# Attention A: the high and the low part of a tile's probabilities turned by two DMA transposes in place of one

## The chip, the core and the metric

The kernel runs on one core of one Trainium2 chip. The metric is the device time of one execution in microseconds. The kernel before has a median of 2229.25 us over three runs (2225.32 to 2232.22).

## What is computed

The program is a chain of four residual blocks on `x` of shape (4, 1024, 128): attention A, a feed-forward block on selected tokens, attention B, and the feed-forward block again. The change touches attention A alone:

```python
logits = jnp.einsum('bhid,bhjd->bhij', q, k) * SCALE      # 16 heads of 8, q and k with rope
logits = jnp.einsum('bhij,gh->bgij', logits, Wpre)        # heads are mixed before the softmax
attn = jax.nn.softmax(logits, axis=-1)
attn = jnp.einsum('bhij,gh->bgij', attn, Wpost)           # and after it
out = jnp.einsum('bhij,bhjd->bhid', attn, v)
out = out.transpose(0, 2, 1, 3).reshape(b, n, DIM)
return out @ Wout.T + bout
```

## The kernel before

`prepare_a` makes q, k (split in two f16 parts, `kh` and `kl`) and v. `attend_a` then works through TILES_A = 512 tiles: 4 batches by 16 mixed heads by 8 tiles of 128 queries. A tile T passes through the engines so:

- TensorE, `scores(T)` (L335): six 512-column matmuls (L349, L350, L353) make 128 x 1024 scores in one of two PSUM buffers, `score_ps[T % 2]`. It waits until the exponential of T-2 is done.
- VectorE, `row_max(T)` (L450): the negated row maximum.
- ScalarE, `exponentiate(T)` (L400): the probabilities `probs`, in f32, and their sum.
- ScalarE, `high(T)` (L408): the high f16 part, `parts[:, T % 4, 0, :]`. It waits until the transpose of tile T-4, which reads the same slot of `parts`, has landed.
- VectorE, `low(T)` (L456): what the high part leaves, in f16, into `parts[:, T % 4, 1, :]`, and the semaphore `lo_ready`.
- SyncE (L326 to L332): one DMA transpose (L330) turns both parts, 128 x 2048 f16, that is 524,288 bytes, into `pT[:, T % 8]`. It waits for `lo_ready` of T and for `pv_done` of T-8, which frees the slot of `pT`.
- TensorE, `times_v(T)` (L357): 24 matmuls of 128 columns. For each of 8 key blocks j it takes high by the high part of v (L367), high by the low part of v (L369) and low by the high part of v (L371).
- ScalarE, `evict` (L418), and GpSimd, `weigh` and `add` (L510, L517), scale and sum two tiles at a time.

The rings are 4 slots deep for `probs` and `parts` (RING_P) and 8 for `pT` (RING_T). TensorE issues `scores(T + 8)` ahead of `times_v(T)`. ScalarE's order is `exponentiate(i)`, then `high(i - 1)`; VectorE's is `row_max(i)`, then `low(i - 2)`. Once in eight tiles, ScalarE and VectorE also make the next head's scaled q (L390, L441).

Of the kernel before, what the change touches and what calls it, by code (L numbers as in the profile page):

```python
# [14 lines left out]
NB, SEQ, D = 4, 1024, 128  # L15
# [12 lines left out]
JB = SEQ // P  # L28
# [3 lines left out]
AHEAD_A, RING_T, RING_P = 8, 8, 4  # L32
# [255 lines left out]
def attend_a(st, io, qT, kh, kl, v, wpre, wpost, acc, pw):  # L288
# [5 lines left out]
    with ExitStack() as s:  # L294
        probs = st.sb(s, "a_probs", [P, RING_P, SEQ])
        parts = st.sb(s, "a_parts", [P, RING_P, 2, SEQ], F16)
        pT = st.sb(s, "a_pT", [P, RING_T, 2, JB, P], F16)
# [5 lines left out]
        vs = st.sb(s, "a_vs", [P, NB, 2, JB, D], F16)  # L303
# [5 lines left out]
        vhi_made, vlo_made, weighed_ready = st.sem("a_vhi_made"), st.sem("a_vlo_made"), st.sem("a_weighed_ready")  # L309
        scored, max_ready, exp_done = st.sem("a_scored"), st.sem("a_max_ready"), st.sem("a_exp_done")  # L310
        hi_ready, lo_ready = st.sem("a_hi_ready"), st.sem("a_lo_ready")
        turned = [st.sem(f"a_turned{i}") for i in range(RING_T)]
        pv_done, rden_ready = st.sem("a_pv_done"), st.sem("a_rden_ready")
        evicted, added = st.sem("a_evicted"), st.sem("a_added")
        block = s.enter_context(nc.Block())

        def wait_turned(eng, T):

            eng.wait_ge(turned[T % RING_T], 16 * (T // RING_T + 1))

        @block.sync
        def _(sp):
            sp.dma_start(pw.ident[:], io["ident"]).then_inc(pw.loaded, 16)
            sp.dma_start(pw.wout[:], io["wout_T"]).then_inc(pw.loaded, 16)
            sp.dma_start(pw.bout[:], io["bout"].broadcast_to([P, D])).then_inc(pw.loaded, 16)
            for T in range(TILES_A):  # L326
                if T >= RING_T:
                    sp.wait_ge(pv_done, T - RING_T + 1)
                sp.wait_ge(lo_ready, T + 1)
                sp.dma_start_transpose(pT[:, T % RING_T].rearrange("p a j q -> p (a j) q"),  # L330
                                       parts[:, T % RING_P].rearrange("p a c -> p (a c)")).then_inc(
                    turned[T % RING_T], 16)  # L332

        @block.tensor
        def _(pe):  # L335
            def scores(T):

                if T >= TILES_A:
                    return
                G, t = T // TPB, T % TPB  # L340
                if t == 0:
                    pe.wait_ge(qlo_made, G + 1)
                if T >= 2:
                    pe.wait_ge(exp_done, T - 1)
                out, base = score_ps[T % 2], G // HA * SEQ
                qhi, qlo = qs[:, G % 2, 0, t * P:(t + 1) * P], qs[:, G % 2, 1, t * P:(t + 1) * P]
                for c in range(2):
                    to, kc = out[:, c * CH:(c + 1) * CH], slice(base + c * CH, base + (c + 1) * CH)
                    pe.matmul(to, qhi, kh[:, kc], start=True, stop=False)  # L349
                    pe.matmul(to, qhi, kl[:, kc], start=False, stop=False)  # L350
                for c in range(2):
                    to, kc = out[:, c * CH:(c + 1) * CH], slice(base + c * CH, base + (c + 1) * CH)
                    last = pe.matmul(to, qlo, kh[:, kc], start=False, stop=True)  # L353
                last.then_inc(scored, 1)

            def times_v(T):

                b = T // (HA * TPB)
                if T % (HA * TPB) == 0:
                    pe.wait_ge(vlo_made, b + 1)  # L360
                if T >= 8 and T % 2 == 0:
                    pe.wait_ge(evicted, T - 6)
                wait_turned(pe, T)
                out = out_ps[:, T // 2 % 4, T % 2, :]
                for j in range(JB):
                    hi, lo = pT[:, T % RING_T, 0, j, :], pT[:, T % RING_T, 1, j, :]
                    pe.matmul(out[:, 0:D], hi, vs[:, b, 0, j, :], start=j == 0, stop=False,  # L367
                              skip_group_check=True)
                    pe.matmul(out[:, 0:D], hi, vs[:, b, 1, j, :], start=False, stop=False,  # L369
                              skip_group_check=True)  # L370
                    last = pe.matmul(out[:, 0:D], lo, vs[:, b, 0, j, :], start=False,  # L371
                                     stop=j == JB - 1, skip_group_check=True)
                last.then_inc(pv_done, 1)

            for T in range(AH):
                scores(T)
            for T in range(TILES_A):
                scores(T + AH)
                times_v(T)

        @block.scalar
        def _(act):
            def scale_q(G):

                if G >= heads:
                    return
                if G >= 2:
                    act.wait_ge(scored, TPB * (G - 1))
                b, g = G // HA, G % HA
                act.activation(qs[:, G % 2, 0, :], qT[:, b * SEQ:(b + 1) * SEQ], ACT.Copy,  # L390
                               scale=wpre[:, g:g + 1]).then_inc(qhi_made, 1)

            def exponentiate(T):

                act.wait_ge(max_ready, T + 1)
                if T >= RING_P:
                    act.wait_ge(lo_ready, T - RING_P + 1)
                if T >= 16:
                    act.wait_ge(rden_ready, T // 2 - 7)
                act.activation(probs[:, T % RING_P, :], score_ps[T % 2][:], ACT.Exp,  # L400
                               bias=negmax[:, T % 8:T % 8 + 1], accum_out=den[:, T % 16:T % 16 + 1]).then_inc(exp_done, 1)

            def high(T):

                act.wait_ge(exp_done, T + 1)
                if T >= RING_P:
                    wait_turned(act, T - RING_P)
                act.activation(parts[:, T % RING_P, 0, :], probs[:, T % RING_P, :], ACT.Copy,  # L408
                               scale=PSCALE).then_inc(hi_ready, 1)

            def evict(pair):

                act.wait_ge(rden_ready, pair + 1)
                act.wait_ge(pv_done, 2 * pair + 2)
                if pair >= 2:
                    act.wait_ge(weighed_ready, pair - 1)
                for T in (2 * pair, 2 * pair + 1):
                    act.activation(own_out[:, T % 4, :], out_ps[:, pair % 4, T % 2, 0:D], ACT.Copy,  # L418
                                   scale=rden[:, T % 16:T % 16 + 1]).then_inc(evicted, 1)

            scale_q(0)
            scale_q(1)
            for i in range(TILES_A + AH + 2):
                if i >= AH + 2 and i % 2 == 0:
                    evict((i - AH - 2) // 2)
                if i < TILES_A:
                    exponentiate(i)
                if 1 <= i <= TILES_A:
                    high(i - 1)
                if i % TPB == 1 and i < TILES_A:  # L430
                    scale_q(i // TPB + 1 if i >= TPB else heads)

        @block.vector
        def _(dve):
# [18 lines left out]
            def low(T):  # L453

                dve.wait_ge(hi_ready, T + 1)
                dve.scalar_tensor_tensor(out=parts[:, T % RING_P, 1, :], in0=probs[:, T % RING_P, :], scalar=PSCALE,  # L456
                                         in1=parts[:, T % RING_P, 0, :], op0=ALU.mult,
                                         op1=ALU.subtract).then_inc(lo_ready, 1)
# [11 lines left out]
            for i in range(TILES_A + AH + 2):  # L470
                if i < TILES_A:
                    row_max(i)
                if 4 <= i < TILES_A + 4 and i % 2 == 0:
                    invert((i - 4) // 2)
                if 2 <= i < TILES_A + 2:
                    low(i - 2)
                if i % TPB == 3 and TPB <= i < TILES_A:
                    low_q(i // TPB + 1)
# [1109 lines left out]
def build(nc, io, out):  # L1588
    with ExitStack() as whole:
# [4 lines left out]
        with ExitStack() as s:  # L1594
            acc = st.sb(s, "acc", [P, NT, D])
            pw = ProjectWeights(st, s)
            with ExitStack() as held:
                qT = st.sb(held, "qT", [P, NTOK])
                kh = st.sb(held, "kh", [P, NTOK], F16)
                kl = st.sb(held, "kl", [P, NTOK], F16)  # L1600
                v = st.sb(held, "v", [P, NTOK])
                wpre = st.sb(held, "wpre", [P, HA])
                wpost = st.sb(held, "wpost", [P, HA * D])
                ident = st.sb(held, "a_ident", [P, P])
                prepare_a(st, io, x, qT, kh, kl, v, wpre, wpost, ident)
                attend_a(st, io, qT, kh, kl, v, wpre, wpost, acc, pw)
            project_a(st, x, acc, pw, lstats, fw)
# [85 lines left out]
```

## Time and profile before

| | |
|---|---|
| median of three runs | 2229.25 us (2225.32 to 2232.22) |
| the profiled execution: its time | 2227.8 us |
| the profiled execution: its span | 2225.9 us |
| mean granted TensorE clock | 0.979 of 2.4 GHz |
| attention A's tiles, first to last DMA transpose issued | 76.6 to 1472.9 us |
| DMA transposes | 512 |

The profile comes from one execution, so a sum over its rows is made against its own 2227.8 us and then carried over to the median, which is 1.45 us longer. In the profile, DVE is VectorE, ACT is ScalarE, POOL is GpSimd, PE is TensorE, PEld its weight load, and SP is SyncE; a q behind an engine's name is its instruction queue. Instructions that only issue a DMA are not counted as busy, so the first part of the page says nothing about SP.

### The profile page before, as it was taken

The page shows a single profiled execution, that of the slowest core. Times are in us where ns is not written, and L with a number is a line of the kernel's source. Part 1 is how long each engine was busy: PE and PEld are TensorE (multiplying, and loading weights), DVE is VectorE, ACT ScalarE, POOL GpSimd, SP SyncE. Part 2 cuts the span into 40 slices and gives each one's busy share as a digit, 9 for nine tenths or more (in the row PEclk, how much of TensorE's full clock was granted, in tenths as well). Part 3 has the DMA queues.
Part 4 walks back from the last instruction along what each step waited for, and adds up shares of the span by engine and source line. Part 5 has one row for each costly group of instructions (what it writes and reads, how often), then busy time and mean ns, then how long its engine had stood idle before and what let it go on. Part 6 is the DMA issues. An engine that isn't in the chain of part 4 may idle for free. (4 is left out here: it accounts for less than half of the span.)

```text
span 2225.9 us, 62041 instructions
## 1 busy us (share of the span) xinstructions
PE 2086.6 (94%) x24854; PEld 1428.7 (64%) x24854; DVE 1905.7 (86%) x2598; ACT 1736.1 (78%) x3088; POOL 876.3 (39%) x958
## 2 busy tenths in 40 slices
PE   6799999999999999999999999978779999999977
PEld 4467776777677777767777767665535555655654
DVE  6899998999999999999999999958677788878684
ACT  3789998999899999989999999943357777777623
POOL 4332332332323323223323233244007777777640
PEclk9999999999999999999999999988989999999988
DMA  3799999999999999999999999970041111111001
GB/s 103 117 199 191 195 196 185 197 194 193 193 191 198 195 192 194 196 192 193 196 195 193 192 194 193 196 136 1 19 154 31 31 31 31 31 31 31 20 1 38
DMA packets 1097038, 303.78 MB, mean 136 GB/s; under 512 B 1070256, under 2 KB 1090096, under 8 KB 1096496
## 3 DMA queue, kind: packets, MB, share of 16 engines
q1 hardware_dynamic: 1095888, 299.36, 77.3%
q8 instruction: 196, 3.21, 0.6%
q14 instruction: 90, 0.74, 0.1%
q10 hardware_dynamic: 864, 0.47, 0.1%
HBM read 20.83 MB, written 10.49 MB: 14 GB/s over the span
## 5 line engine op out<-in xcount | busy, mean ns | idle before, releaser
L456 DVE SCALAR_TENSOR_TENSOR a_parts<-a_probs,a_parts 128x1024 f16<-128x1024 f32 x512 | 659.2, 1287 | 81.3 <-ACT a_parts L408 80.3
L367 PE MATMUL a_out_ps<-a_vs,a_pT 128*128 128x128 f16 x4096 | 713.5, 219 | 3.8 <-DMA a_pT<-a_parts 3.8
L369 PE MATMUL a_out_ps<-a_vs,a_pT 128*128 128x128 f16 x4096 | 713.5, 219 | 0.0
L371 PE MATMUL a_out_ps<-a_vs,a_pT 128*128 128x128 f16 x4096 | 713.5, 219 | 0.0
L400 ACT ACTIVATE a_probs<-a_score_ps,a_negmax 128x1024 f32<-128x1024 f32 x512 | 570.8, 1115 | 94.1 <-DVE a_negmax L450 86.4
L450 DVE TENSOR_REDUCE a_negmax<-a_score_ps 128x1 f32<-128x1024 f32 x512 | 621.5, 1214 | 9.9 <-PE a_score_ps L353 7.6
L510 POOL TENSOR_TENSOR a_weighed<-a_own_out,wpost 128x256 f32<-128x256 f32 x256 | 246.7, 964 | 965.3 <-DVE a_parts L456 959.7
L408 ACT ACTIVATE a_parts<-a_probs 128x1024 f16<-128x1024 f32 x512 | 540.0, 1055 | 34.0 <-DMA a_pT<-a_parts 32.5
L367 PEld LDWEIGHTS a_out_ps<-a_vs,a_pT 128*128 128x128 f16 x4096 | 401.3, 98 | 63.5 <-ACT a_own_out L418 3.1
L369 PEld LDWEIGHTS a_out_ps<-a_vs,a_pT 128*128 128x128 f16 x4096 | 401.2, 98 | 59.4
L349 PE MATMUL a_score_ps<-kh,a_qs 128*128 128x512 f16 x1024 | 390.1, 381 | 44.2 <-ACT a_probs L400 35.3
L371 PEld LDWEIGHTS a_out_ps<-a_vs,a_pT 128*128 128x128 f16 x4096 | 401.3, 98 | 0.0
L350 PE MATMUL a_score_ps<-kl,a_qs 128*128 128x512 f16 x1024 | 388.9, 380 | 0.0
L771 POOL TENSOR_TENSOR b_sums<-b_probs 128x512 f32<-128x512 f32 x256 | 323.2, 1274 | 105.5 <-ACT b_probs L689 105.5
L741 DVE TENSOR_REDUCE b_negmax<-b_max_ps 128x1 f32<-128x1024 f32 x256 | 297.4, 1203 | 37.2 <-PE b_max_ps L607 37.2
L689 ACT ACTIVATE b_probs<-b_score_ps 128x512 f32<-128x512 f32 x512 | 264.6, 603 | 81.5 <-PE b_score_ps L634 79.9
L353 PE MATMUL a_score_ps<-kh,a_qs 128*128 128x512 f16 x1024 | 305.0, 379 | 0.0
L517 POOL TENSOR_TENSOR acc<-acc,a_weighed 128x256 f32<-128x256 f32 x256 | 185.6, 725 | 0.0
L349 PEld LDWEIGHTS a_score_ps<-kh,a_qs 128*128 128x128 f16 x1024 | 100.1, 98 | 126.5 <-ACT a_probs L400 54.7
L353 PEld LDWEIGHTS a_score_ps<-kh,a_qs 128*128 128x128 f16 x1024 | 100.3, 98 | 121.2 <-issue 0.8
L418 ACT ACTIVATE a_own_out<-a_out_ps,a_rden 128x128 f32<-128x128 f32 x512 | 157.7, 363 | 10.0 <-PE a_out_ps L371 5.4
L607 PE MATMUL b_max_ps<-b_ks,b_qs 96*128 96x512 f16 x512 | 156.4, 388 | 9.6 <-DMA b_ks<-k_parts 8.6
(233 smaller groups left out, 2234.7 us busy)
## 6 DMA issues: line engine op xcount, KB each, us to landing
a_pT<-a_parts SPq DMA_TRANSPOSE x512, 5.1
b_qs<-q_parts SPq DMA_DIRECT2D x96, 64.0 KB, 1.9
b_ks<-k_parts SPq DMA_DIRECT2D x96, 64.0 KB, 1.9
q_parts<-b_parts SPq DMA_DIRECT2D x32, 128.0 KB, 1.9
k_parts<-b_parts SPq DMA_DIRECT2D x32, 128.0 KB, 1.8
x<-x_dram SPq DMA_DIRECT2D x4, 512.0 KB, 7.5
a_rope<-rope_dram SPq DMA_DIRECT2D x1, 2048.0 KB, 11.7
out_dram<-x SPq DMA_DIRECT2D x4, 512.0 KB, 5.4
```

The costliest lines, as they stand in the source:

```text
L349: pe.matmul(to, qhi, kh[:, kc], start=True, stop=False)
L350: pe.matmul(to, qhi, kl[:, kc], start=False, stop=False)
L353: last = pe.matmul(to, qlo, kh[:, kc], start=False, stop=True)
L367: pe.matmul(out[:, 0:D], hi, vs[:, b, 0, j, :], start=j == 0, stop=False, skip_group_check=True)
L369: pe.matmul(out[:, 0:D], hi, vs[:, b, 1, j, :], start=False, stop=False, skip_group_check=True)
L371: last = pe.matmul(out[:, 0:D], lo, vs[:, b, 0, j, :], start=False, stop=j == JB - 1, skip_group_check=True)
L400: act.activation(probs[:, T % RING_P, :], score_ps[T % 2][:], ACT.Exp, bias=negmax[:, T % 8:T % 8 + 1], accum_out=den[:, T % 16:T % 16 + 1 ...
L408: act.activation(parts[:, T % RING_P, 0, :], probs[:, T % RING_P, :], ACT.Copy, scale=PSCALE).then_inc(hi_ready, 1)
L450: dve.tensor_reduce(negmax[:, T % 8:T % 8 + 1], score_ps[T % 2][:], AX.X, ALU.max, negate=True).then_inc(max_ready, 1)
L456: dve.scalar_tensor_tensor(out=parts[:, T % RING_P, 1, :], in0=probs[:, T % RING_P, :], scalar=PSCALE, in1=parts[:, T % RING_P, 0, :], op0 ...
L741: dve.tensor_reduce(negmax[:, u % 2, t:t + 1], max_ps[n % 2][:], AX.X, ALU.max, negate=True).then_inc(max_ready, 1)
L771: pool.tensor_tensor(sums[:, u % 2, pair, :], probs[:, u % 2, 2 * pair, :], probs[:, u % 2, 2 * pair + 1, :], ALU.add).then_inc(added, 1)
```

## The change

Each tile gets two DMA transposes: one of the high part as soon as `hi_ready` comes, one of the low part after `lo_ready`. Each part has its own set of eight semaphores. `high(T)` waits for the landing of the high half of T-4 only; `low(T)` gets a wait of its own for the low half of T-4. `times_v` waits for the high half, issues the 16 products with it, then waits for the low half and issues the other 8. The bytes, the matmuls and the rings are the same.

```diff
-        turned = [st.sem(f"a_turned{i}") for i in range(RING_T)]
+        turned_hi = [st.sem(f"a_turned_hi{i}") for i in range(RING_T)]
+        turned_lo = [st.sem(f"a_turned_lo{i}") for i in range(RING_T)]
...
-        def wait_turned(eng, T):
+        def wait_turned(eng, turned, T):
             eng.wait_ge(turned[T % RING_T], 16 * (T // RING_T + 1))
...
                 if T >= RING_T:
                     sp.wait_ge(pv_done, T - RING_T + 1)
+                sp.wait_ge(hi_ready, T + 1)
+                sp.dma_start_transpose(pT[:, T % RING_T, 0], parts[:, T % RING_P, 0, :]).then_inc(
+                    turned_hi[T % RING_T], 16)
                 sp.wait_ge(lo_ready, T + 1)
-                sp.dma_start_transpose(pT[:, T % RING_T].rearrange("p a j q -> p (a j) q"),
-                                       parts[:, T % RING_P].rearrange("p a c -> p (a c)")).then_inc(
-                    turned[T % RING_T], 16)
+                sp.dma_start_transpose(pT[:, T % RING_T, 1], parts[:, T % RING_P, 1, :]).then_inc(
+                    turned_lo[T % RING_T], 16)
...
-                wait_turned(pe, T)
+                wait_turned(pe, turned_hi, T)
                 out = out_ps[:, T // 2 % 4, T % 2, :]
                 for j in range(JB):
-                    hi, lo = pT[:, T % RING_T, 0, j, :], pT[:, T % RING_T, 1, j, :]
-                    pe.matmul(out[:, 0:D], hi, vs[:, b, 0, j, :], start=j == 0, stop=False,
-                              skip_group_check=True)
-                    pe.matmul(out[:, 0:D], hi, vs[:, b, 1, j, :], start=False, stop=False,
-                              skip_group_check=True)
-                    last = pe.matmul(out[:, 0:D], lo, vs[:, b, 0, j, :], start=False,
+                    for a in range(2):
+                        pe.matmul(out[:, 0:D], pT[:, T % RING_T, 0, j, :], vs[:, b, a, j, :], start=j == 0 and a == 0,
+                                  stop=False, skip_group_check=True)
+                wait_turned(pe, turned_lo, T)
+                for j in range(JB):
+                    last = pe.matmul(out[:, 0:D], pT[:, T % RING_T, 1, j, :], vs[:, b, 0, j, :], start=False,
                                      stop=j == JB - 1, skip_group_check=True)
                 last.then_inc(pv_done, 1)
...
                 if T >= RING_P:
-                    wait_turned(act, T - RING_P)
+                    wait_turned(act, turned_hi, T - RING_P)
...
                 dve.wait_ge(hi_ready, T + 1)
+                if T >= RING_P:
+                    wait_turned(dve, turned_lo, T - RING_P)
```

## Rows read from the trace of the kernel before

**Rows 1.** The head of the page, with busy time by engine.
```profile
span 2225.9 us, 62041 instructions
...
PE 2086.6 (94%) x24854; PEld 1428.7 (64%) x24854; DVE 1905.7 (86%) x2598; ACT 1736.1 (78%) x3088; POOL 876.3 (39%) x958
```

**Rows 2.** Who waited for whom, 300 to 1400 us: total us, times, longest.
```profile
ACT a_probs L400 <- DVE a_negmax L450: 65.1, 125, 1.1
DVE a_parts L456 <- ACT a_parts L408: 63.5, 91, 1.9
...
ACT a_parts L408 <- DMA a_pT<-a_parts: 25.5, 47, 1.6
PE a_score_ps L349 <- ACT a_probs L400: 24.3, 66, 1.0
```

**Rows 3.** Timeline from 700 us, TensorE: start, length, first products of two tiles.
```profile
702.66 0.22 PE L367 MATMUL a_out_ps<-a_vs,a_pT 128*128 128x128 f16 x1
...
702.72 0.22 PE L369 MATMUL a_out_ps<-a_vs,a_pT 128*128 128x128 f16 x1
...
705.29 0.22 PE L367 MATMUL a_out_ps<-a_vs,a_pT 128*128 128x128 f16 x1
```

**Rows 4.** SyncE: its timeline, 300 to 1400 us; the DMA transposes' own view, same window.
```profile
299.60 1101.96 SPq L330 DMA_TRANSPOSE a_pT<-a_parts  x403
...
L330 SPq DMA_TRANSPOSE a_pT<-a_parts x403: 1698/2502/3928, 299.6 to 1398.3; - x135
...
DMA to landing us min/median/max: 4.2/5.1/7.1
```

**Rows 5.** What writes and reads `parts`, 60 to 703.3 us: counts, durations, first and last start.
```profile
L456 DVE SCALAR_TENSOR_TENSOR a_parts<-a_probs,a_parts x231: 1201/1226/1458, 75.4 to 701.6; 128x1024 f16<-128x1024 f32 x116
L330 SPq DMA_TRANSPOSE a_pT<-a_parts x229: 1698/2483/3928, 76.6 to 699.2; - x115
```

**Rows 6.** SyncE's timeline: start and length of single transposes.
```profile
643.20 2.55 SPq L330 DMA_TRANSPOSE a_pT<-a_parts  x1
645.85 2.18 SPq L330 DMA_TRANSPOSE a_pT<-a_parts  x1
648.12 2.56 SPq L330 DMA_TRANSPOSE a_pT<-a_parts  x1
650.77 2.26 SPq L330 DMA_TRANSPOSE a_pT<-a_parts  x1
653.12 3.30 SPq L330 DMA_TRANSPOSE a_pT<-a_parts  x1
```

**Rows 7.** Windows of 0.25 us: length, granted clock, DMA share, GB/s.
```profile
627.00:627.25 0.25, 1.00 1.15 216
627.25:627.50 0.25, 1.00 1.13 183
627.50:627.75 0.25, 1.00 0.99 142
627.75:628.00 0.25, 1.00 1.14 228
628.00:628.25 0.25, 1.00 1.19 249
...
631.00:631.25 0.25, 1.00 1.49 11
631.25:631.50 0.25, 1.00 0.00 0
...
632.25:632.50 0.25, 1.00 0.09 13
...
633.00:633.25 0.25, 1.00 1.27 290
...
635.75:636.00 0.25, 1.00 0.97 170
636.00:636.25 0.25, 1.00 0.33 61
```

**Rows 8.** DMA queues, 300 to 1400 us: packets, MB, share.
```profile
q8 instruction: 95, 1.56, 0.5%
q14 instruction: 44, 0.36, 0.1%
```

**Rows 9.** SyncE's timeline behind the stage: one plain DMA issued.
```profile
1484.05 0.43 SPq L820 DMA_DIRECT2D fw_g<-g_dram  x1
```

**Rows 10.** Who waited for whom, 1460 to 1500 us, the stage's end.
```profile
PE a_out_ps L367 <- DMA a_pT<-a_parts: 3.8, 2, 3.0
```

## The prediction

> **What bounds the kernel now.** The page's head [rows 1] shows TensorE busy for 94% of the span, and a first reading makes it the bound. The view of waits for the middle of attention A [rows 2] shows that it is not there: TensorE waits for the exponential, ScalarE for the row maximum and for a transpose that has to free a slot of `parts`, VectorE for ScalarE. A ring of engines that wait for each other has its cause elsewhere, so I look for something without a gap. TensorE's own work for a tile is the distance from one tile's first product to the next where nothing interrupts it, 705.29 - 702.66 = 2.63 us [rows 3]. The tiles come at 1101.96 / 403 = 2.73 us [rows 4]. TensorE is thus 0.10 us a tile faster than the stage.
>
> SyncE's timeline settles it. The 403 transposes of the window are one unbroken row [rows 4]. Single ones follow each other 0.09 us after the end of the one before: 643.20 + 2.55 = 645.75, and the next starts at 645.85 [rows 6]. Nor does SyncE wait for its data: by 703.3 us VectorE had started 231 low parts, the last at 701.6, while only 229 transposes had been issued [rows 5]. The 230th low part was therefore complete before 701.6, and SyncE, still in the transpose before it, took it up only after 703.3. So the transposes are the bound of the stage, 512 of them at 2.73 us. The waits of the other engines are back-pressure from a full `parts` ring.
>
> What does a transpose spend its time on? A tile's 524,288 bytes at the steady 216 to 218 GB/s (I use 217 [rows 7]) are 2.42 us. Undisturbed starts lie (653.12 - 643.20) / 4 = 2.48 us apart [rows 6]. So some 0.06 us a tile belongs to the seam between two transposes. From there to 2.73 it is pauses: the traffic falls to nothing for over a microsecond [rows 7], about once in three tiles (95 + 44 instruction fetches against 403 transposes [rows 4, 8]; that the fetches are the cause is my reading, the row shows only that the counts are alike). After a pause the queue catches up at 290 GB/s [rows 7]. Pauses cost 2.73 - 2.48 = 0.25 us a tile net, 128 us in all.
>
> **The change part by part.**
>
> *One more transpose a tile, the same bytes.* The bytes still need 2.42 us. What is doubled is the seam. Three readings of one: the 0.06 us above; the dip at 627.25 to 628.25, where 183, 142, 228 and 249 GB/s against 217 lack 66 x 0.25 = 16.5 KB, or 0.08 us; and the dip at 635.75, where 170 and 61 lack 203 x 0.25 = 51 KB, or 0.23 us [rows 7]. Their mean is 0.12 us, my value: 512 x 0.12 = +61 us. The bounds from these rows are 0.06 and 0.23, so +31 and +118 us. Below that, a half might cost no seam at all; a gain I exclude for this term, since no byte goes away.
>
> *SyncE's own share of an instruction.* The trace has no transpose of another size, so this must be bounded. From below it is nothing, if SyncE writes ahead of the transfers. From above it is what a small DMA takes to issue, 0.43 us [rows 9], with the 0.05 us step to the next: +0.48 us a tile, +246 us, if nothing hides it. Which end is nearer? The shortest transpose held SyncE for 1.70 us [rows 4], so SyncE's own work in one is at most that. With its gap and the second instruction it comes to 1.70 + 0.09 + 0.48 = 2.27 us, under the 2.48 us that the transfers need. I take it as hidden in undisturbed stretches: 0. The cover is the 0.21 us between them, and it is thin where the queue catches up after a pause (below).
>
> *Three more waits and one more issue to fetch.* All instructions fetched in the window are 1.92 MB for 403 tiles [rows 4, 8], 4.8 KB a tile. A tile gains a transpose and waits on SyncE, TensorE and VectorE, four instructions. The window's groups hold about 75 instructions a tile by my count of the code (60 on TensorE with the weight loads). That is 5% more to fetch; 5% of the 128 us of pauses is +6 us. Nothing below 0, at most twice that.
>
> *TensorE's new order and wait.* 24 products as before, each with a weight load as before and 0.055 to 0.06 us after the one ahead of it [rows 3]: 0. The wait for the low half stands in front of 8 products and then `scores(T + 9)`. In the whole stage TensorE waited for a transpose only at its very end [rows 10], so the wait finds its half landed. Its cover is 2.73 + 0.12 against 2.63 us of work.
>
> *VectorE's new wait, ScalarE's looser one.* `high(T)` can be free earlier, since the high half lands first; that takes away some of the 25.5 us of waits for the transpose [rows 2], and returns nothing, because the tiles it would hasten stand in the same queue. Behind VectorE's wait stand `row_max(T + 3)`, the exponential that needs it, and `scores(T + 5)`. These will wait more, as the queue is slower than they are. On the path they cost nothing beyond the queue's own time.
>
> *The ends of the stage.* The first half can be issued when the first high part is ready, ahead of the low part by one VectorE operation of 1.2 us [rows 5]. At the end TensorE waits up to 3.0 us for a transpose [rows 10]; 16 of 24 products can now go ahead of the last landing, 0.9 us at 0.055. Together -2 us.
>
> The sum is +61 + 6 - 2 = +65 us. On the profiled execution that is 2227.8 + 65 = 2292.8 us; on the median, which is 1.45 us longer, **2294 us**, 2.9% slower. A tile would take about 2.86 us.
>
> **A rule weighed.** The rows show 217 GB/s in an undisturbed transpose [rows 7]. By the code, one tile's source has 4,096 contiguous bytes in each partition (two parts of 1024 f16 side by side), and each half 2,048. The Trainium skill ("DMA: Bandwidth & Descriptors", section "Latency and other measured facts") says that a DMA transpose loses about 30% of its bandwidth where it can't join 4 KB of reading, and gives 261 GB/s against 350 to 400. The trace's 217 is already below both figures, so I think that the penalty, if it is one of this kind, is paid now. The same page ("Rules for kernel authors") advises joining small transfers and calls those under 64 KB mostly overhead; a half here has 256 KB, and the seam read above is what the advice would come to.
>
> **The rivals.**
>
> *SyncE becomes the bound, at least after pauses.* A pause is longer than what it costs: the traffic all but stops for about 1.4 us (11 GB/s from 631.00, 0 from 631.25, 13 up to 632.50 [rows 7]), at 139 fetches in 403 tiles 0.48 us a tile, and 0.25 is the net cost. The rest, 0.23 us, is won back at 290 GB/s, which needs SyncE to feed a tile in 1.8 us. With two instructions of up to 2.27 us it could not. If all of the recovery is lost, that is 512 x 0.23 = +118 us on top of the forecast, 2412 us; the outer bound, with the 0.48 us all unhidden in place of the seam, is 2229 + 246 = 2475. For it: 0.43 us for even a small DMA [rows 9]. Against it: the 0.43 us may lie within the transfer of the half ahead.
>
> *The early high half pays: faster.* If the two halves together need no more than TensorE's 2.63 us a tile, TensorE becomes the bound, and the looser slots of `parts` take away the waits in the ring. The price is 512 x (2.73 - 2.63) = -51 us, 2178 us. It decides only from 2.63 us for a tile's two halves, pauses included, which means that halves would have to be transferred faster than one whole. The one thing for it is that the low rate lies at a transpose's end [rows 7], which might be an effect of its length.
>
> *No change.* The seam belongs to the bytes, not to the instruction, or it lies hidden behind what is queued: 2229 us, within 0.3%, 2223 to 2236.
>
> *Shorter rows are read more slowly.* If 2,048 bytes in a partition in place of 4,096 lower the rate of the transfers by 30%, the 2.42 us become 3.45, +1.03 us a tile, 512 x 1.03 = +527 us: 2756 us. This is what the skill's figures would make of it, too. Against it is the rate of now.
>
> **How the numbers follow.** The forecast, with its seam between 0.06 and 0.23 us (2255 to 2350 us, its own range), has 0.59. SyncE as the bound, 2350 to 2475, has 0.22; no change 0.08; faster 0.07; shorter rows 0.04. About 0.3% is what can be told from no change. Slower by more than that is 0.59 + 0.22 + 0.04 = 0.85; same 0.08; faster 0.07. The range takes the forecast, half of the case without a change and most of the one with SyncE as the bound: 2230 to 2420 us, which leaves about 2 in 10 out.
>
> **What would show it.** In the profile after: 1024 transposes on SyncE, again without gaps, an undisturbed pair at 2.60 us and all at 2.86; two dips a tile in the GB/s, each like today's one, between stretches at 217; TensorE with more idle time in the stage; VectorE and ScalarE waiting for transposes for the difference. If single halves take SyncE much more than 1.25 us and the GB/s between the dips are below 217, or it no longer reaches 290 after a pause, SyncE is the bound. Gaps in SyncE's row would show that a wait for `hi_ready` or `lo_ready` holds the queue, and the account would be wrong from its start. Outside attention A nothing should move by more than a microsecond.

## The result

The kernel after has a median of 2340.32 us (2332.88 to 2342.77, four runs) against 2229.83 us (2225.32 to 2232.22, four runs) for the kernel before: ratio 1.049, 95% interval 1.0469 to 1.0511. The change costs 110 us. The time lies in the predicted range and on the predicted side, 46 us above the predicted 2294 us.

**The profile after.** The head of the page:

```profile
span 2337.4 us, 63061 instructions
...
PE 2103.1 (90%) x24854; PEld 1429.8 (61%) x24854; DVE 1897.4 (81%) x2598; ACT 1750.8 (75%) x3088; POOL 876.0 (37%) x958
```

The work on the engines has hardly changed [rows 1], and every share of busy time has fallen: TensorE is busy for 16.5 us more and ScalarE for 14.7, VectorE for 8.3 less, so nobody got much more to do, and all wait more. The view of waits, 300 to 1400 us (total us, times, longest), shows whom they wait for:

```profile
PE a_score_ps L352 <- ACT a_probs L403: 95.5, 128, 2.6
ACT a_parts L411 <- DMA a_pT<-a_parts: 88.1, 107, 2.2
DVE a_parts L461 <- ACT a_parts L411: 80.1, 82, 2.0
DVE a_parts L461 <- DMA a_pT<-a_parts: 72.9, 98, 2.4
ACT a_probs L403 <- DVE a_negmax L453: 69.5, 121, 1.3
```

ScalarE waited 25.5 us for the transpose of a slot before [rows 2]; now it is 88.1, although its own wait is for the high half alone, and VectorE's new wait adds 72.9. The slots come free later, not earlier. The transposes' own view of the same window (durations min/median/max in ns, first and last start):

```profile
L334 SPq DMA_TRANSPOSE a_pT<-a_parts x372: 1231/1337/2746, 298.8 to 1397.3; - x186
L331 SPq DMA_TRANSPOSE a_pT<-a_parts x372: 1231/1286/2527, 300.3 to 1398.7; - x186
...
DMA to landing us min/median/max: 3.2/3.4/5.5
```

This is where the time is. A tile now comes every (1397.3 - 298.8) / 371 = 2.96 us; it was 2.73 [rows 4]. And the durations have changed in kind: the whole transposes lay anywhere between 1.70 and 3.93 us with a median of 2.50, so they followed the traffic; the halves have their median within 0.11 us of their minimum. SyncE's timeline, single transposes (start, length), high half L331 and low half L334:

```profile
634.20 1.33 SPq L334 DMA_TRANSPOSE a_pT<-a_parts  x1
635.63 1.28 SPq L331 DMA_TRANSPOSE a_pT<-a_parts  x1
636.95 1.34 SPq L334 DMA_TRANSPOSE a_pT<-a_parts  x1
638.39 1.26 SPq L331 DMA_TRANSPOSE a_pT<-a_parts  x1
...
645.21 2.00 SPq L334 DMA_TRANSPOSE a_pT<-a_parts  x1
```

Between pauses a pair takes (645.21 - 634.20) / 4 = 2.75 us where the whole took 2.48 [rows 6]: 1.28 and 1.33 us of transposes, 0.05 us ahead of the low one and 0.09 to 0.10 ahead of the high one, which has two semaphores to wait for. The traffic in windows of 0.25 us (length, granted clock, DMA share, GB/s):

```profile
628.75:629.00 0.25, 1.00 0.86 162
629.00:629.25 0.25, 1.00 0.70 146
629.25:629.50 0.25, 1.00 1.05 217
...
630.25:630.50 0.25, 1.00 0.59 122
...
632.25:632.50 0.25, 1.00 0.07 6
...
633.25:633.50 0.25, 1.00 1.28 291
...
634.00:634.25 0.25, 1.00 0.56 108
```

There are two dips a tile, with stretches at 200 to 217 GB/s between them, and a pause as before. What differs from before [rows 7] is what comes behind a pause: the queue ran on at 290 GB/s before; now it falls from 291 to 108 within a microsecond.

The sum closes. The first transpose starts at 74.5 us (76.6 before) and the last at 1587.1 (1472.9 before). From first to last that is 1512.6 against 1396.3 us, +116.3. The start is 2.1 us earlier, and from the last transpose to the end of the span are 750.3 us against 753.0, 2.7 less. 116.3 - 2.1 - 2.7 = 111.5 us, the difference of the spans, 2337.4 - 2225.9.

### The profile page after: what moved, and what is told of

The parts are those of the page before. It is cut to its first block and busy times, and to the rows that moved or that the text cites. A ratio compares the mean times of both kernels' runs of the same rounds, so it can differ in the third digit from the quotient of the medians.

```text
span 2337.4 us, 63061 instructions
## 1 busy us (share of the span) xinstructions
PE 2103.1 (90%) x24854; PEld 1429.8 (61%) x24854; DVE 1897.4 (81%) x2598; ACT 1750.8 (75%) x3088; POOL 876.0 (37%) x958
## 5 line engine op out<-in xcount | busy, mean ns | idle before, releaser
L461 DVE SCALAR_TENSOR_TENSOR a_parts<-a_probs,a_parts 128x1024 f16<-128x1024 f32 x512 | 642.6, 1255 | 205.9 <-ACT a_parts L411 106.5
L370 PEld LDWEIGHTS a_out_ps<-a_vs,a_pT 128*128 128x128 f16 x8192 | 502.7, 98 | 124.8 <-ACT a_own_out L421 2.6
L370 PE MATMUL a_out_ps<-a_vs,a_pT 128*128 128x128 f16 x8192 | 543.9, 220 | 4.8 <-DMA a_pT<-a_parts 4.8
L374 PE MATMUL a_out_ps<-a_vs,a_pT 128*128 128x128 f16 x4096 | 313.2, 219 | 0.9 <-DMA a_pT<-a_parts 0.7
L374 PEld LDWEIGHTS a_out_ps<-a_vs,a_pT 128*128 128x128 f16 x4096 | 250.9, 98 | 1.6 <-DMA a_pT<-a_parts 1.6
L639 PE MATMUL b_score_ps<-b_qs,b_ks 128*128 128x512 f16 x512 | 156.2, 382 | 1.1 <-ACT b_probs L694 0.7
L651 PE MATMUL b_out_ps<-b_probs,b_v_all 128*32 128x128 f32 x4096 | 138.3, 276 | 0.0
```

The lines of the kernel that those rows point to most:

```text
L370: pe.matmul(out[:, 0:D], pT[:, T % RING_T, 0, j, :], vs[:, b, a, j, :], start=j == 0 and a == 0, stop=False, skip_group_check=True)
L374: last = pe.matmul(out[:, 0:D], pT[:, T % RING_T, 1, j, :], vs[:, b, 0, j, :], start=False, stop=j == JB - 1, skip_group_check=True)
```

## The experiments

Each ratio below is taken against the kernel before as it ran beside that version, 2227.22, 2226.94 or 2224.75 us at the median. Three theories stood at the start. S: each transpose costs SyncE a time of its own, so their number is what counts. T: the seam between transfers costs the DMA engines time, whatever SyncE does. O: the order of the products, or the split waits, cost it.

**One part alone: the order of the products.**

```diff
                 for j in range(JB):
-                    hi, lo = pT[:, T % RING_T, 0, j, :], pT[:, T % RING_T, 1, j, :]
...
+                    for a in range(2):
+                        pe.matmul(out[:, 0:D], pT[:, T % RING_T, 0, j, :], vs[:, b, a, j, :], start=j == 0 and a == 0,
+                                  stop=False, skip_group_check=True)
+                for j in range(JB):
+                    last = pe.matmul(out[:, 0:D], pT[:, T % RING_T, 1, j, :], vs[:, b, 0, j, :], start=False,
                                      stop=j == JB - 1, skip_group_check=True)
```

> One transpose a tile as before; only the order of the 24 products is that of the change (16 with the high part, then 8 with the low part). Theory S (the number of transposes costs the time) and its rival T (the seam between transfers costs it) both expect no change: 2229 us within 0.3%, a tile every 2.73 us. A third theory, O (the product order costs TensorE time or the new wait drains it), expects most of the +110 us here.

2226.78 us against 2227.22, ratio 1.000 (0.9991 to 1.0009). Order costs nothing, and O has lost its first half.

**The other part alone: two transposes.**

```diff
-            eng.wait_ge(turned[T % RING_T], 16 * (T // RING_T + 1))
+            eng.wait_ge(turned[T % RING_T], 32 * (T // RING_T + 1))
...
+                flat = parts[:, T % RING_P].rearrange("p a c -> p (a c)")
+                rows = pT[:, T % RING_T].rearrange("p a j q -> p (a j) q")
+                for lo, hi in ((0, 8), (8, 16)):
+                    sp.dma_start_transpose(rows[:, lo:hi, :], flat[:, lo * P:hi * P]).then_inc(
+                        turned[T % RING_T], 16)
```

> Two transposes of half the columns a tile, both issued after the low part is ready, on one semaphore with doubled count; product order and all other waits as before. S and T expect the whole loss of the change: 2340 us within 8 us, and the same pair time on SyncE, 2.76 us undisturbed. O, or a theory that the split waits cause it, expects 2229 to 2260 us.

2340.09 us, ratio 1.0502 (1.0486 to 1.0518): the whole loss, with the old order, the old waits and no early high half. Its transposes look like those of the change:

```profile
L333 SPq DMA_TRANSPOSE a_pT<-a_parts x745: 1231/1332/2807, 298.6 to 1399.8; - x187
```

O is refuted. S and T are still level.

**Four quarters.** The same with `((0, 4), (4, 8), (8, 12), (12, 16))` and a count of 64.

> Four transposes of a quarter each, otherwise as the one with two. S says that SyncE has a fixed time F in each transpose plus a part that goes with the bytes: F + P/2 = 1.28 us as in the change's halves, and F + P at most the 1.70 us of the shortest whole, so F is at least 0.86 and a quarter takes at least 1.07 us: 4 x 1.12 to the next = 4.5 us a tile or more, about 3250 us or more. T says that each further seam costs the transfers 0.28 us whatever SyncE does: 2.48 + 3 x 0.28 = 3.32 us undisturbed, about 2229 + 430 = 2660 us, with the traffic at 217 GB/s between the seams.

3622.16 us, ratio 1.6252 (1.6227 to 1.6276).

```profile
L333 SPq DMA_TRANSPOSE a_pT<-a_parts x810: 1188/1267/2576, 299.5 to 1399.2; - x162
```

A quarter holds SyncE for 1.27 us, a half for 1.28 to 1.34. The time of a small transpose is nearly all fixed. The view of its DMA queues, same window (packets, MB, share of the 16 engines):

```profile
q1 hardware_dynamic: 440247, 106.17, 52.2%
```

The same queue had 115.5% before. At 52% the DMA engines aren't full, so it isn't the transfers that set the pace. T, which expected 2660 us, is out. S named a lower bound, 3250; a time of some 1.27 us for a quarter and not 1.07 explains the rest: 4 x (1.27 + 0.05) = 5.3 us undisturbed, and a tile took 4 x (1399.2 - 299.5) / 809 = 5.44.

**An uneven split**, with `((0, 4), (4, 16))`, 512 and 1536 columns.

> Two transposes a tile of 512 and 1536 columns in place of 1024 and 1024, otherwise as the one with two halves. S with a time that is linear in the bytes expects the same sum, 2.76 us a tile undisturbed and 2340 us; SyncE would hold 1.07 and 1.5 us for them. If small transposes have a floor of about 1.28 us and the large one is paced by the transfers, the sum is about 1.28 + 1.85 = 3.1 us, 2229 + 330 = 2560 us. T expects 2340 us.

2516.72 us, ratio 1.1295 (1.1276 to 1.1314).

```profile
L333 SPq DMA_TRANSPOSE a_pT<-a_parts x670: 1202/1515/2805, 299.6 to 1398.6; - x168
```

A tile takes 2 x (1398.6 - 299.6) / 669 = 3.29 us, pauses included, though the bytes and the number of transposes are those of the two halves, which take 2.96. Neither S nor T in their simple form allows this: the sum over a tile would be the same. The sum fits a rule that I call the lock-step: SyncE can be one transpose ahead of the transfers and no more, so each step costs the longer of SyncE's 1.31 us (1.27 and 0.05 to the next) and the transfer of the one ahead. For two halves that is SyncE's time twice, since 1.21 us of bytes fit under it; here it is 1.31 over the small piece, and over the large one its 2.42 x 3/4 = 1.82 us and a seam, 3.15 us in all, with 0.14 left for the pauses.

The single rows do not bear the rule out, though. By it the small piece, issued while the large one ahead is transferred, would hold SyncE for some 1.8 us, and the large one behind it for 1.27. Two tiles in a row between pauses (start, length); the first piece of a tile, the small one, starts 0.10 us after the row before it, because of its semaphore waits, and the large one 0.04:

```profile
633.66 1.55 SPq L333 DMA_TRANSPOSE a_pT<-a_parts  x1
635.25 1.50 SPq L333 DMA_TRANSPOSE a_pT<-a_parts  x1
636.85 1.52 SPq L333 DMA_TRANSPOSE a_pT<-a_parts  x1
638.42 1.51 SPq L333 DMA_TRANSPOSE a_pT<-a_parts  x1
```

A tile takes 638.42 - 635.25 = 3.17 us, which is the rule's sum, but both pieces hold SyncE for about 1.5. The lock-step is thus a formula for the sum of a tile, and not shown as the mechanism.

**A forecast from the lock-step: three pieces**, `((0, 2), (2, 4), (4, 16))` and a count of 48.

> Three transposes a tile of 256, 256 and 1536 columns. Lock-step (a transpose can't be set up by SyncE more than one ahead of the transfer, so each step costs the longer of 1.31 us and the transfer ahead): 1.31 + 1.31 + 1.85 = 4.47 us undisturbed, with 0.2 us of pauses 4.65 us a tile, about 2229 + 985 = 3210 us. If SyncE and the transfers ran freely side by side, the larger of 3 x 1.31 = 3.93 us and 2.42 us of bytes plus seams: 3.95 to 4.1 us a tile with pauses, 2850 to 2930 us.

3181.94 us, ratio 1.43 (1.4269 to 1.4332).

```profile
L333 SPq DMA_TRANSPOSE a_pT<-a_parts x718: 1168/1492/2892, 299.6 to 1400.0; - x180
```

3 x (1400.0 - 299.6) / 717 = 4.60 us a tile. The lock-step had said 4.65 and 3210 us, free running 2850 to 2930, so free running is out. The sum is again the lock-step's, and its division again is not. The two small pieces and the large one of a tile (start, length):

```profile
641.80 1.47 SPq L333 DMA_TRANSPOSE a_pT<-a_parts  x1
643.31 1.25 SPq L333 DMA_TRANSPOSE a_pT<-a_parts  x1
644.60 1.52 SPq L333 DMA_TRANSPOSE a_pT<-a_parts  x1
```

The rule would have some 1.8, 1.27 and 1.27 us. Nor does the time by itself single the rule out: the uneven split's 3.29 us and one more small transpose at 1.31 are 4.60 us, too.

**A half by itself.** Only the high part is turned; the 8 products with the low part read the high part's columns in its place, so TensorE's work is whole and the low part's share of the sum is left out.

```diff
-                sp.dma_start_transpose(pT[:, T % RING_T].rearrange("p a j q -> p (a j) q"),
-                                       parts[:, T % RING_P].rearrange("p a c -> p (a c)")).then_inc(
+                sp.dma_start_transpose(pT[:, T % RING_T, 0], parts[:, T % RING_P, 0, :]).then_inc(
                     turned[T % RING_T], 16)
...
-                    hi, lo = pT[:, T % RING_T, 0, j, :], pT[:, T % RING_T, 1, j, :]
+                    hi, lo = pT[:, T % RING_T, 0, j, :], pT[:, T % RING_T, 0, j, :]
```

> Only the high part is transposed, one transpose of half the bytes a tile; the 8 products with the low part read the high part's columns instead, so their sum is another one. Theory S, now as a lock-step of two stages (SyncE's own work of about 1.25 us in each transpose, and the transfer of the one ahead): a half takes 1.3 us against a tile's 2.63 us of TensorE, so the queue is idle half the time, a single transpose still holds SyncE for 1.2 to 1.3 us, and the stage falls to TensorE's 2.63 us a tile: 2229 - 51 = 2178 us, 2170 to 2190. If the 1.28 us of a half are the transfers' pace, it falls clearly below 1.2 us with an empty queue. If the stage isn't bound by the queue, 2229 us.

2195.01 us, ratio 0.9853 (0.9832 to 0.9875).

```profile
L330 SPq DMA_TRANSPOSE a_pT<-a_parts x411: 1231/1232/2582, 300.8 to 1398.6; - x137
...
DMA to landing us min/median/max: 3.0/3.1/5.3
```

This measures the disputed cost: with nothing ahead of it in the queue, a transpose of 256 KB holds SyncE for 1.232 us at the median and 1.231 at the least. It also shows what the stage is without the bound: a tile every (1398.6 - 300.8) / 410 = 2.68 us, 0.05 above TensorE's 2.63. I had expected 2178 us; the missing 17 us lie within that 0.05 a tile (26 us), waits of the compute engines for each other that remain.

**The opposite of the change: one transpose for two tiles.** 1 MB each, 256 in all, with `parts` six slots deep.

```diff
-AHEAD_A, RING_T, RING_P = 8, 8, 4
+AHEAD_A, RING_T, RING_P, RING_F = 8, 8, 6, 4      # RING_F: slots of probs
...
-            eng.wait_ge(turned[T % RING_T], 16 * (T // RING_T + 1))
+            eng.wait_ge(turned[T % RING_T // 2], 16 * (T // RING_T + 1))
...
+                if T % 2 == 0:
+                    continue
                 if T >= RING_T:
                     sp.wait_ge(pv_done, T - RING_T + 1)
                 sp.wait_ge(lo_ready, T + 1)
+                at, of = (T - 1) % RING_T, (T - 1) % RING_P
+                sp.dma_start_transpose(pT[:, at:at + 2].rearrange("p t a j q -> p (t a j) q"),
+                                       parts[:, of:of + 2].rearrange("p t a c -> p (t a c)")).then_inc(
+                    turned[at // 2], 16)
```

> The opposite of the change: one transpose for two tiles, 1 MB, 256 in all, with parts 6 slots deep (probs stays 4) so that a slot still comes free in time. Lock-step: only the seam of 0.06 us is halved, 0.03 us a tile: -15 us, 2214 us. If each transpose costs the 0.28 us of seam that the halves showed, 0.14 us a tile: -72 us, limited by TensorE's 2.63 us to 2178 us. If the longer wait for two tiles starves the queue or the slots: slower than 2229 us, with gaps in SyncE's row.

2201.4 us, ratio 0.9887 (0.9869 to 0.9904): this version beats both kernels. Its transposes in the window:

```profile
L333 SPq DMA_TRANSPOSE a_pT<-a_parts x207: 4797/5013/5909, 296.9 to 1399.8; - x104
...
who waited for it (us, times):
  PE a_out_ps L370: 0.2, 1
```

And two of its waits there:

```profile
PEld a_score_ps L352 <- ACT a_probs L403: 17.4, 50, 0.4
...
PE a_score_ps L352 <- ACT a_probs L403: 8.8, 50, 0.2
```

A tile takes (1399.8 - 296.9) / 412 = 2.68 us, the same as with half of the bytes left out. ScalarE has no wait for a transpose left, and TensorE's wait is down from 24.3 to 8.8 us. The stage has passed from the queue to the compute engines, by 25.5 us and not by my 15. The shortest pair holds SyncE for 4.80 us, with its gap 2.45 us a tile, 0.03 less than a whole; how the rest of the gain divides between seams and pauses isn't shown. The waits of the compute engines are nearly those of the run with half of the bytes, where TensorE waited 9.0 us for the exponential.

**The control: six slots alone.**

```diff
-AHEAD_A, RING_T, RING_P = 8, 8, 4
+AHEAD_A, RING_T, RING_P, RING_F = 8, 8, 6, 4
```

> The kernel before with parts 6 slots deep and nothing else, the control of the run with pairs. The queue is the bound, so a deeper ring only moves the waits: no change, 2229 us within 0.3%, and fewer waits of ScalarE for the transpose. If the slots were the bound: up to -51 us.

2229.06 us, ratio 1.0011 (0.9998 to 1.0024). The waits for transposes go over from ScalarE, which had 25.5 us [rows 2], to TensorE:

```profile
PEld a_out_ps L367 <- DMA a_pT<-a_parts: 28.0, 39, 1.9
PE a_out_ps L367 <- DMA a_pT<-a_parts: 20.2, 44, 1.4
ACT a_parts L408 <- DMA a_pT<-a_parts: 10.5, 22, 1.1
```

So the slots gave nothing by themselves; the gain comes with the pairs.

**The change with its number of transposes undone.** The high parts of two tiles in one transpose, their low parts in another: separate waits, the high part ahead of the low and the new order stay, 512 transposes of 512 KB as before. `parts` is six slots deep here. The diff is cut, and its first line is a note.

```diff
 # the kernel after, with parts [P, RING_P // 2, 2, 2, SEQ] and pT [P, RING_T // 2, 2, 2, JB, P]
+                to, of = T % RING_T // 2, T % RING_P // 2      # odd T only
                 sp.wait_ge(hi_ready, T + 1)
+                sp.dma_start_transpose(pT[:, to, 0].rearrange("p t j q -> p (t j) q"),
+                                       parts[:, of, 0].rearrange("p t c -> p (t c)")).then_inc(
+                    turned_hi[to], 16)
                 sp.wait_ge(lo_ready, T + 1)
+                sp.dma_start_transpose(pT[:, to, 1].rearrange("p t j q -> p (t j) q"),
+                                       parts[:, of, 1].rearrange("p t c -> p (t c)")).then_inc(
+                    turned_lo[to], 16)
```

> The change's separate transposes, waits and product order, but with as many transposes as before: the high parts of two tiles in one, their low parts in another, 512 KB each, 512 in all; parts 6 slots deep. Lock-step: it is the number that costs, so 2229 us within 10 us. If it is the separation of the parts (its waits, its order, the halves' places) that costs: most of the +110 us, near 2340 us. If the earlier high part brings anything, below 2220 us.

2231.66 us, ratio 1.0023 (1.0013 to 1.0034).

```profile
L338 SPq DMA_TRANSPOSE a_pT<-a_parts x201: 1777/2488/4127, 299.3 to 1396.4; - x101
L334 SPq DMA_TRANSPOSE a_pT<-a_parts x201: 1812/2502/3992, 302.0 to 1398.5; - x101
```

All but 5 of the 110 us are gone with the extra transposes, and an early high part, as far as a pair allows one, brings nothing. The six slots aren't the reason, as the last run shows.

**Pairs of tiles with the old four slots.** The kernel with pairs as above, `RING_P = 4`.

> One transpose for two tiles, as in the run that gained, but with parts at its old 4 slots. A slot is free only when the pair's transpose, up to 7.5 us from issue to landing, is over, and one pair is filled while the other is turned: the queue should run dry between transposes. Expected: slower than with 6 slots (2201 us), gaps in SyncE's row and waits of ScalarE for the transpose; a pair then takes about 7.5 us of landing plus the 2.4 us or more in which the next pair's parts are completed, shared over two overlapping pairs: 2300 to 2700 us. If the slots don't matter: 2201 us.

2502.74 us, ratio 1.1248 (1.1221 to 1.1274).

```profile
L333 SPq DMA_TRANSPOSE a_pT<-a_parts x170: 4774/4876/5658, 295.5 to 1398.3; - x170
...
who waited for it (us, times):
  ACT a_parts L411: 217.2, 121
```

A pair now takes (1398.3 - 295.5) / 169 = 6.53 us, of which the transpose holds SyncE for 4.88: the queue runs dry for 1.6 us until the next pair of slots has been freed and filled. The larger transpose pays only with the two slots that cover its time to landing.

**The change with six slots.** The same `RING_P = 6` in the kernel after.

> The change with parts 6 slots deep. The waits of ScalarE and VectorE for the halves, 88 and 73 us in the profile of the change, are back-pressure if the queue is the bound: they shrink or move to TensorE, and the time stays at 2340 us within 8 us. If the slots of parts cost the time in the change, up to -110 us.

2330.99 us, ratio 1.0475 (1.0453 to 1.0498), an interval that overlaps the one of the change. That is 9 us under its 2340, one more than I had allowed; but the kernel before, too, had 2224.75 us beside it and not 2229.83. ScalarE's waits for the halves are down from 88.1 to 49.4 us and VectorE's from 72.9 to 21.2, and TensorE now waits 49.7 and 35.7 us for them. The slots aren't what costs time here either.

## Why the prediction was right, and which step was not

The side and the range came out; the sum behind 2294 us did not, and some of the agreement is luck. The forecast put the loss into a seam between transfers and took SyncE's time as hidden. The runs show the mechanism of the rival that had 0.22: SyncE's time for the extra transpose is what costs. That 2340 us lies even in the forecast's own 2255 to 2350 us comes from an upper bound that I had read off the deepest dip in the traffic, 0.23 us, which measures something else.

**Transposes as the bound of the stage: right.** With fewer of them the stage is faster and with more it is slower, with every other engine's work the same. One of the arguments for it was worth less than I made of it, though: that the timeline shows all of a window's transposes as one row. It merges them whatever lies between. The run with the high part only has such a row, too:

```profile
300.76 1099.08 SPq L330 DMA_TRANSPOSE a_pT<-a_parts  x411
```

yet 411 times 1.23 us are 506 us of 1099. What carried the argument are the single rows, 0.09 us apart [rows 6], and the low parts that stood ready before their transpose was taken up [rows 5]. In that example SyncE was not "still in the transpose before" to the end: that one ran from 699.18 to 702.98 us, and the next started at 703.40. The part had been ready since before 701.6 us, so this gap of 0.42 us was not a wait for it.

**The seam, +61 us: the step that failed, by its size and by its cause.** I put 0.12 us a tile on the second transpose, as time of the transfers; between pauses it costs 2.75 - 2.48 = 0.27 us, 512 x 0.27 = +138 us, outside even my upper bound of 0.23. The reason lies one paragraph further on.

**SyncE's own time hidden, 0: wrong.** From a plain DMA's 0.43 us [rows 9] I took 0.48 us for what a second transpose asks of SyncE, and got 2.27 us a tile, under the 2.48 of the transfers. Measured, a half asks for 1.23 us with an empty queue and 1.28 to 1.34 with a full one, and two of them with their gaps are the 2.75 us. A plain DMA is no measure for a transpose: the 1.70 us of the shortest whole one held as a bound for one transpose, but the 0.48 us for a second was the error. For a whole transpose the 1.2 us lie under 2.42 us of transfer and cost nothing that a run shows; for a half they lie over 1.21. Even the empty queue's time gives 2 x 1.23 + 0.05 + 0.09 = 2.60 us a tile, above the 2.48 of the wholes; the other 0.15 us up to 2.75 are the longer rows in a full queue, and why these are longer isn't shown. That is the rival in which SyncE becomes the bound; it had 0.22 and 2350 to 2475 us, and the time came out 10 us below it. My sign for it was a poor one: halves that hold SyncE for "much more than 1.25 us", when 1.28 to 1.34 is enough. The profile after could not settle it by that sign; the quarters and the half by itself did.

**The recovery after pauses, lost in that rival: not lost.** Pauses cost 2.96 - 2.75 = 0.21 us a tile after and 0.25 before, 20 us less in all. The stretch at 290 GB/s is shorter, and still a pause costs no more than before; a queue paced by SyncE has less to catch up with, but that is only my reading. +138 - 20 are the 116 us between the first and the last transpose, but for 2.

**Instruction fetches, +6 us: in the right order, but not separable.** The queues of instructions in the window:

```profile
q8 instruction: 88, 1.44, 0.5%
q14 instruction: 48, 0.39, 0.1%
```

1.83 MB in 372 tiles are 4.9 KB a tile against 4.8 [rows 4, 8], 3% and not 5. That the pauses are these fetches was never tested.

**The products' order, TensorE's wait, the slots: right at 0.** The order alone gave a ratio of 1.000; VectorE's new wait is 72.9 us long and costs nothing, since more slots, which shorten it, leave the time where it was.

**The ends, -2 us: right in sign,** -4.8 us by the sum above.

**Shorter rows: right at 0.** The wholes ran at 216 to 218 GB/s and the halves at 200 to 217 between the dips. The transposes' DMA queue from 300 to 1400 us (packets, MB, share of 16 engines), before and after:

```profile
q1 hardware_dynamic: 837277, 211.10, 115.5%
q1 hardware_dynamic: 784656, 194.88, 107.5%
```

Both are 0.55% a MB: a byte took the transfers as long in a half as in a whole. The 30% for short reading that the Trainium skill states ("DMA: Bandwidth & Descriptors", "Latency and other measured facts") doesn't show between these two. The Trainium skill's advice to join small transfers (same page, "Rules for kernel authors") holds here, and well above the 64 KB under which it calls them mostly overhead: halves of 256 KB lost 4.9%, and 1 MB with six slots gained 1.1% over 512 KB.

What stays open: the lock-step's formula fits the time of a tile in halves, quarters, the uneven split and three pieces, but not how that time divides between the pieces. What on the way from SyncE to the transfers holds SyncE back beside a large transpose, no run shows. Nor is it known why the traffic stops every few tiles.

## What to carry to other kernels

A queue that only issues is missing from the list of busy engines, and it can still be the bound. Read its single instructions: gaps of under 0.1 us and data that was ready before are the sign. Where a DMA transpose is on the path, it has a nearly fixed price at its issuer, here at least 1.2 us each. At 512 KB this lay under 2.42 us of transfer; at 256 KB, with 1.21 us of transfer, the price set the pace. An estimate of the size between them is 280 KB (1.31 us at 217 GB/s), which no run tried. So before a transfer is split to start its first half sooner, ask whether anyone waits for that half; if the queue is full, join transfers in place of splitting them, and add the slots that the longer time to landing needs. And split evenly if at all: 128 and 384 KB cost more than 256 and 256.

## What the runs showed of the hardware that was not expected

- A small DMA transpose from SBUF to SBUF holds SyncE for nearly the same time whatever its size: 1.25 us for 64 KB behind another, 1.27 us at the median for 128 KB, 1.23 us for 256 KB alone in the queue. A plain DMA issue took 0.43 us [rows 9].
- A small transpose next to a large one costs more than two of middle size, 3.29 against 2.96 us a tile for the same bytes. Between pauses the 128 and the 384 KB then hold SyncE for about 1.5 us each.
- In the run with quarters, TensorE's granted clock was 0.83 at the mean between 300 and 500 us, that is partly below the 2.4 GHz level, with TensorE busy for 131 of the 200 us. In the change it stayed at 1.00, the 2.4 GHz level, in the same stretch with 182 us busy, so its 110 us hold no loss of clock there.
